# Steps of attention in pairs, a third buffer of probabilities, and a last block in halves

## What is computed

```python
xn = _ln(x, ln1_g, ln1_b)
q, k, v = split(xn @ w_in.T + b_in)              # 16 heads
allowed = (idx % STRIDE == 0)[:, None] | (idx[:, None] == idx[None, :])   # STRIDE = 8
attn = softmax(where(allowed, q @ k.T / sqrt(16), -inf))
x1 = x + (attn @ v) @ w_out.T + b_out
block = x1 + gelu(_ln(x1, ln2_g, ln2_b) @ w1.T + b1) @ w2.T + b2
```

## Time and profile before

| | |
|---|---|
| time, median of 3 runs | 1542.11 us (1539.95 to 1959.27) |
| the profiled execution | 1542.38 us, span 1540.6 us, mean granted clock 0.979 |
| TensorE busy | 1438.3 us, 93% |
| VectorE, ScalarE, GpSimd busy | 835.1, 724.8, 654.2 us |
| attention 0 to 3 | 185.2 to 342.6, 523.3 to 708.1, 885.5 to 1070.3, 1247.2 to 1402.6 us |
| tail | 1402.6 to 1540.6 us |

### The profile page before, as it was taken

One profiled execution on the slowest core, in us unless ns is written; L12 is line 12 of the kernel. 1 busy time (PEld: TensorE's weight loads), 2 busy tenths in 40 slices (PEclk: granted clock), 3 DMA queues, 4 the chain that ended last, 5 costly groups with the idle time before them and its releaser, 6 DMA issues.

```text
span 1540.6 us, 26428 instructions
## 1 busy us (share of the span) xinstructions
PE 1438.3 (93%) x10166; PEld 1077.8 (70%) x10166; DVE 835.1 (54%) x1786; ACT 724.8 (47%) x1071; POOL 654.2 (42%) x536
## 2 busy tenths in 40 slices
PE   4799899999989999999999999999999999999886
PEld 3587655568878765668888866557887865557776
DVE  6655566635745465545646555653664647652331
ACT  3244455553434555554444455454344455554432
POOL 1464411237754422244864431324775422134545
PEclk9899999999999999999999999999999999999999
DMA  7565123205561131212672213220566122300100
GB/s 186 159 197 133 35 47 71 54 16 168 188 161 56 36 75 31 67 43 69 196 205 61 76 24 74 51 52 21 185 191 148 42 55 59 58 24 29 55 1 28
DMA packets 102974, 132.08 MB, mean 86 GB/s; under 512 B 18889, under 2 KB 79249, under 8 KB 99729
## 3 DMA queue, kind: packets, MB, share of 16 engines
q1 hardware_dynamic: 102848, 130.39, 31.3%
HBM read 68.87 MB, written 61.36 MB: 85 GB/s over the span
## 4 chain that ended last, share of the span: by engine, by line
PE 75%; DVE 9%; POOL 5%; SPq 3%; issue 2%; ACT 2%; DMA 2%; POOLq 0%; DVEq 0%; ACTq 0%
PE ps L1370 18%; PE ps L1372 15%; PE ps L1371 15%; PE ps L1546 8%; PE ps L1535 6%; PE ps L1520 5%; DVE mx L1283 2%; PE ps L1591 2%; PE ps L1610 2%; PE ps L1582 2%; POOL rows L922 2%; SPq L747 1%; PE ps L1552 1%; DVE stats L1165 1%; DMA k_d<-kst 1%
## 5 line engine op out<-in xcount | busy, mean ns | idle before, releaser
L1283 DVE TENSOR_REDUCE mx<-ps 128x2 f32<-128x1024 f32 x256 | 313.1, 1223 | 266.6 <-PE ps L1520 252.1
L1033 ACT ACTIVATE prob<-ps 128x1024 f32<-128x1024 f32 x256 | 261.8, 1023 | 155.7 <-PE ps L1535 155.3
L931 POOL TENSOR_TENSOR hid1l<-gel,hid1h 128x512 fp32r<-128x512 f32 x85 | 110.9, 1305 | 233.6 <-ACT hid1h L1075 233.6
L931 POOL TENSOR_TENSOR hid0l<-gel,hid0h 128x512 fp32r<-128x512 f32 x86 | 112.5, 1308 | 226.0 <-ACT hid0h L1075 226.0
L931 POOL TENSOR_TENSOR hid2l<-gel,hid2h 128x512 fp32r<-128x512 f32 x85 | 111.0, 1306 | 223.1 <-ACT hid2h L1075 223.1
L1067 ACT ACTIVATE gel<-ps,cols 128x512 f32<-128x512 f32 x128 | 88.2, 689 | 198.8 <-PE ps L1372 190.3
L1546 PE MATMUL ps<-prob,vals 128*32 128x256 f32 x2048 | 166.3, 397 | 0.0
L1069 ACT ACTIVATE gel<-ps 128x512 f32<-128x512 f32 x128 | 76.5, 597 | 179.7 <-PE ps L1610 179.7
L1535 PE MATMUL ps<-qslot,kslot 50*128 50x256 f32 x1024 | 131.2, 335 | 6.7 <-ACT prob L1033 6.4
L1535 PEld LDWEIGHTS ps<-qslot,kslot 50*128 50x128 f32 x1024 | 77.9, 188 | 73.0 <-issue 47.8
L1520 PE MATMUL ps<-kslot,qslot 48*128 48x512 f32 x512 | 109.7, 424 | 9.0 <-DVE mx L1283 5.9
(11 more groups left out here) (230 smaller groups left out, 3966.7 us busy)
## 6 DMA issues: line engine op xcount, KB each, us to landing
k_d<-kst SPq DMA_DIRECT2D x192, 128.0 KB
kslot<-k_d SPq DMA_DIRECT2D x64, 384.0 KB
xin<-in_L_attn_x SPq DMA_DIRECT2D x32, 256.0 KB, 4.1
x1in<-x_d SPq DMA_DIRECT2D x16, 512.0 KB, 6.8
rows<-xs_d SPq DMA_DIRECT2D x16, 512.0 KB, 5.6
out<-rows SPq DMA_DIRECT2D x16, 512.0 KB, 3.5
y_d<-rows SPq DMA_DIRECT2D x15, 512.0 KB, 3.1
rows<-y_d SPq DMA_DIRECT2D x15, 512.0 KB, 4.3
```

The lines of the kernel that those rows point to most:

```text
L931: nc.gpsimd.tensor_tensor(hid[i % RING][1][:], gel[i % 2][:], hid[i % RING][0][:], ALU.subtract).then_inc(lo_done, 1)
L1033: nc.scalar.activation(prob[(n - 1) % 2][:].rearrange("p e i q -> p (e i q)"), ps[:, 0:2, :].rearrange("p a n -> p (a n)"), ACT.Exp).then_ ...
L1283: nc.vector.tensor_reduce(best[:, :, j % NQ], ps[:, MX:MX + 2, :], AX.X, ALU.max).then_inc(maxr_done, 1)
```

## The change

- Attention: sc and mx of a step stay together, but the weighted sums of two steps stand as one group ahead of the odd step's scores: sc(s), mx(s), at(s-2), at(s-1), sc(s+1), mx(s+1). Both steps of a pair are released together, then three parts of items follow (two where there are two blocks). A third `prob` buffer lies on the two x1 output buffers `x1o`; ACT and GpSimd get waits for that. `ot` is asked for at the second key step everywhere.
- Tail: for batch 3, `opj` writes x1 of tile column 0 straight into `x1in`; only the other half is loaded, and early. `l2a`, `l2b` and the turns move into items 4 to 7 of the first block.
- The last block: sum, statistics, power, normalization (now on VectorE) and store go in halves (`fa`, `fb`).

```diff
-            if p and kk == (1 if len(blocks) == 2 else 3):
+            if p and kk == 1:
...
         def step(s):
+            if s % 2:
+                weighted(s - 3)
+                weighted(s - 2)
             scores(s)
             maxima(s)
-            weighted(s - 1)
             turns(s)
             moves(s)
...
-            while s < STEPS_B and s * 4 * n <= (quarter + ahead) * STEPS_B:
+            while s < STEPS_B and (s - s % 2) * 4 * n // STEPS_B <= quarter + ahead:
...
+        weighted(STEPS_B - 2)
         weighted(STEPS_B - 1)
...
-        items(first, {0: chain[0], 1: chain[1], 2: chain[2], 3: chain[3], 4: [("l2l", middle)], 5: [("ld", middle)], 7: [("l2a", middle)]}, first - 1)
-        put(("l2b", middle))
-        put(("tn", middle, 0))
-        put(("tn", middle, 1))
+        items(first, {0: [("l2l", middle)] + chain[0], 1: chain[1], 2: chain[2], 3: chain[3], 4: [("l2a", middle)],
+                      5: [("ld", middle), ("l2b", middle)], 6: [("tn", middle, 0)], 7: [("tn", middle, 1)]}, first - 1)
...
-        drain()
-        put(("la", last))
-        put(("lb", last))
-        put(("st", last))
+        while pending:
+            i = pending.pop(0)
+            put(("dn", i, 0))
+            put(("dn", i, 1))
+        for h in range(2):
+            put(("fa", h))
+        for h in range(2):
+            put(("fb", h))
...
-        prob = [place(f"prob{i}", [P, 2, 2, QW], F32, m0 + 4096 * i)[0] for i in range(2)]
+        prob = [place(f"prob{i}", [P, 2, 2, QW], F32, at)[0] for i, at in enumerate((m0, m0 + 4096, r1 + 8192))]
...
+                    if n == 0 and bb == LAST:
+                        sp.dma_start(tiles_of(x1in[:])[:, :, 1, :], x1_d[bb, :, :, 1, :]).then_inc(x1ld, 16)
...
+                    if b and PLACE[c] < 2:
+                        pool.wait_ge(av_done, N("at", b - 1, PAIRS - 1, KK - 1))
...
+                    elif a[1:] == (0, 2):
+                        for c in (CHUNKS[-3], CHUNKS[-1]):
+                            k, v = X1_STORE[(b, c)]
+                            act.wait_ge(x1st[k], v)
                     else:
-                        act.wait_ge(av_done, n - 2)
+                        act.wait_ge(av_done, n - 3)
...
+                elif what == "fa":
+                    h = a[0]
+                    pool.wait_ge(fvare_done, h + 1)
+                    nc.gpsimd.tensor_tensor(arstd[:, h, :], avare[:, h, :], mhalf[:, 0:AT], ALU.pow).then_inc(frstd_done, 1)
...
+                    x1 = tiles_of(x1in[:])[:, :, 0, :] if b == LAST else x1g[:]
+                    nc.vector.tensor_tensor(x1, x1g[:], ps[:, BANK[(what, *a)], :].rearrange("p (t d) -> p t d", t=NQ), ALU.add
...
+                elif what == "fa":
+                    h = a[0]
+                    k = len(BLOCKS) - 1
+                    y = rows[ROW_OF[k]][:, 2 * h:2 * h + 2, :]
+                    dve.wait_ge(half_done if h == 0 else down_done, FT * (k + 1))
+                    nc.vector.tensor_tensor(flat(y), flat(y), ps[:, DOWN + h, :], ALU.add).then_inc(fsum_done, 1)
...
+                elif what == "fb":
+                    h = a[0]
+                    y = rows[ROW_OF[len(BLOCKS) - 1]]
+                    dve.wait_ge(frstd_done, h + 1)
+                    for t in range(AT):
+                        at = AT * h + t
+                        nc.vector.tensor_scalar(y[:, at, :], y[:, at, :], amv[:, h, t, 0:1], arstd[:, h, t:t + 1],
+                                                ALU.subtract, ALU.mult).then_inc(fnorm_done, 1)
```

More of the change, by code:

```diff
@@ L21 @@
 KT = D // P
+LAST = B - 1
 FT = F // P
@@ L806, in step @@
                     _, bb, n = BLOCKS[a[0]]
-                    if n == 0:
+                    if n == 0 and bb < LAST:
                         sp.wait_ge(x1gst, 16 * N("stg", bb))
@@ L819, in step @@
                         sp.wait_ge(av_done, N("at", last, PAIRS - 1, KK - 1))
-                    sp.dma_start(tiles_of(x1in[:]), x1_d[bb, :, :, 2 * n:2 * n + 2, :]).then_inc(x1ld, 16)
+                    if n == 0 and bb == LAST:
+                        sp.dma_start(tiles_of(x1in[:])[:, :, 1, :], x1_d[bb, :, :, 1, :]).then_inc(x1ld, 16)
+                    else:
+                        sp.dma_start(tiles_of(x1in[:]), x1_d[bb, :, :, 2 * n:2 * n + 2, :]).then_inc(x1ld, 16)
                 elif what == "ld":
@@ L837, in step @@
                     sp.dma_start(tiles_of(rows[k][:]), src[bb, :, :, 2 * n:2 * n + 2, :]).then_inc(rld[k], 16)
+                elif what == "fb":
+                    h = a[0]
+                    _, bb, n = BLOCKS[-1]
+                    sp.wait_ge(fnorm_done, AT * (h + 1))
+                    sp.dma_start(o_v[bb, :, h, 2 * n:2 * n + 2, :], rows[ROW_OF[len(BLOCKS) - 1]][:, 2 * h:2 * h + 2, :]).then_inc(fst, 16)
                 elif what == "st":
@@ L1329, in step @@
                     dve.wait_ge(xgc_done, N("ldg", b))
-                    nc.vector.tensor_tensor(flat(x1g[:]), flat(x1g[:]), ps[:, BANK[(what, *a)], :], ALU.add).then_inc(x1g_done, 1)
+                    x1 = tiles_of(x1in[:])[:, :, 0, :] if b == LAST else x1g[:]
+                    nc.vector.tensor_tensor(x1, x1g[:], ps[:, BANK[(what, *a)], :].rearrange("p (t d) -> p t d", t=NQ), ALU.add
+                                            ).then_inc(x1g_done, 1)
                 elif what == "l2a":
                     dve.wait_ge(x1ld, 16 * N("l2l", *a))
+                    if PHASE[a[0]][0] == "tail":
+                        dve.wait_ge(x1g_done, N("opj", LAST))
                     ln_a(LN[("l2a", *a)], x1in)
                 elif what == "l2b":
+                    if PHASE[a[0]][0] == "tail":
+                        dve.wait_ge(xsg_done, N("opj", LAST))
                     ln_b(LN[("l2a", *a)], x1in)
@@ L1359, in step @@
                     pick(*a)
+                elif what == "fa":
[3 more added lines that the diff above has]
+                    dve.wait_ge(half_done if h == 0 else down_done, FT * (k + 1))
+                    if h == 0:
+                        dve.wait_ge(xw_done, N("xw", k))
+                    nc.vector.tensor_tensor(flat(y), flat(y), ps[:, DOWN + h, :], ALU.add).then_inc(fsum_done, 1)
+                    dve.wait_ge(fsum_done, h + 1)
+                    for t in range(AT):
+                        nc.vector.bn_stats(astats[:, h, t, :], y[:, t, :]).then_inc(fstat_done, 1)
+                    dve.wait_ge(fstat_done, AT * (h + 1))
+                    for t in range(AT):
+                        nc.vector.bn_aggr(amv[:, h, t, :], astats[:, h, t, :]).then_inc(faggr_done, 1)
+                    dve.wait_ge(faggr_done, AT * (h + 1))
+                    nc.vector.tensor_scalar(avare[:, h, :], amv[:, h, :, 1], EPS, None, ALU.add).then_inc(fvare_done, 1)
+                elif what == "fb":
+                    h = a[0]
+                    y = rows[ROW_OF[len(BLOCKS) - 1]]
+                    dve.wait_ge(frstd_done, h + 1)
+                    for t in range(AT):
+                        at = AT * h + t
+                        nc.vector.tensor_scalar(y[:, at, :], y[:, at, :], amv[:, h, t, 0:1], arstd[:, h, t:t + 1],
+                                                ALU.subtract, ALU.mult).then_inc(fnorm_done, 1)
             for s in STEPS:
```

14 lines of the change are left out of this document (9 added, 5 removed).

## The result

The changed kernel takes 1561 us in the median (1556.6 to 1570.7) beside 1541 for the kernel before: a ratio of 1.0139, 95% interval 1.0113 to 1.0165. The change is some 20 us slower, and 1567 with a range of 1540 to 1592 had been forecast. The profiled execution has a span of 1562.3 us, 21.7 more than before.

The account below looks back on a forecast made before the run. TensorE's own order was taken to set the end in attention. Terms -9 +12.6 +20 +4 +4 -3 -4 = +24.6 us, added to the span of 1540.6 and 1.8 around it, gave 1567 us; range 1540 to 1592.

Parts of the forecast that it names:

- Grouping: Attention: two steps in one group save 0.04 to 0.05 us a pair with maxima; -9 us over all pairs.
- The end of the pair: Attention: items start 2.60 us after a pair's first scores, 0.43 + 0.11 behind the second maxima.
- the second sum: Attention: one weighted sum behind another costs about 0.24 us instead of 0.57.
- rival 1: Attention: grouping pays in full, 0.40 us a pair, 51 us; with the tail, 1484 us; chance 0.05.
- mt without its cover: Attention 0 and 3: turns of negated maxima directly follow turns of blocks and wait longer, 6.3 us a stage, +12.6.
- Bursts: Attention: VectorE's other work falls between pairs and delays reductions, so maxima wait; +20 us, bounds 0 and 40.
- First exponentials: Attention 1 and 2: nothing lies between first and second scores, which wait 1.9 us more each; +4 us.
- Clock: Attention 1 and 2: half clock behind the first exponential's bare wait, 0 to 3.4 us each; +4 us together.
- rival 3: Attention: waits grow into each other or the clock falls there too; above 1590 us; chance 0.10.
- Tail and last block: After attention: x1 skips the trip through memory, -3 us; last block's work in halves, -4 us.
- Third buffer: Attention: second exponential needn't wait for weighted sums, a wait that isn't there now; worth nothing by itself.
- Rival 2: Attention: VectorE's late work is absorbed and the clock holds; +0.6 us, 1543 us; chance 0.25.

Follow-up runs that it names:

- b_pairs: The kernel before with only the edits of attention (steps in pairs, third buffer), its tail as before: 1566.8 us, ratio 1.0171.
- a_tail: The changed kernel with all of attention undone, keeping only the new tail and last block: 1533.3 us, ratio 0.995.
- g_half_after: The changed kernel with exponential and maxima reduction over half of the columns each (doesn't compute the layer): 1512.9 us, ratio 0.9821.
- k_first_apart: The changed kernel with mt ahead of an item's third-part products, and the first two steps of attention 1 and 2 apart: 1526.3 us, ratio 0.9912.
- i_best: The kernel before's attention order with the new tail, mt ahead of third-part products, x1's statistics and turns one item earlier: 1513.7 us, ratio 0.982.
- c_buffer: The kernel before with only the third buffer of probabilities, its index and waits: 1539.3 us, ratio 0.9983.

## Why the prediction was right

**The account.** Forecast: attention +31.6, tail -3, last block -4, in all +24.6. Measured alone: attention +27 (`b_pairs`), tail with last block -6.5 (`a_tail`), and +20 together. The direction and the reason held; three terms inside attention were off, and that the sum came so near is in part luck, since their errors cancel.

**Grouping, -9 forecast, about -19.5 by the rows** (it was not measured alone). The distances were right: scores follow scores after 1.62 to 1.68 us in the pairs, maxima follow maxima after 1.71. The reason for the second was right too; for the first it was only half right, since TensorE's own work is as long (`g_half_after`). The end of the pair was mis-sized. I added 0.11 for late weights to a distance of 0.43 that already had it; and 1.23 from one step's scores to the item was right. The pair takes 2.48 and not 2.60, so 0.16 is saved and not 0.045: 96 x 0.16 = 15.4, and about 4.2 for the pairs without maxima as forecast. The other mistake, 0.24 instead of 0.43 for the second sum, put the end of the sums at 1.47, where it is 1.66. By luck it did not enter the sum: 1.66 lies only 0.04 behind the exponential's 1.62, and the second maxima wait for the reduction until 2.05 in any case. It made rival 1 too good: of its 0.40 a pair, at most 0.18 + 0.14 was ever there.

**mt without its cover, +12.6 forecast, +12.7 measured** (8.8 to 21.5 by line). Behind the turns of a block it waits 1.4 us each time, four times in attention 3, as the waits above show and as predicted.

**Bursts, +20 forecast, +13.1 measured** (5.9 to 19.0; the stage of the earlier trace rows 4.7 instead of 2.4, that of the earlier trace rows 5.0 instead of 0.5). I had 7 a stage. Fewer bursts come late than I placed, and one came later than forecast: where the negated maxima, the sum and the statistics of a block fall into one window, I had 1.3 and it is 2.63. Timelines of attention 1, VectorE and then TensorE:

```profile
608.19 1.09 DVE L1327 CAST negs<-negm 128x4 fp32r<-128x4 f32 x1
...
609.39 1.28 DVE L1389 TENSOR_TENSOR rows<-rows,ps 128x512 f32<-128x512 f32 x2
610.71 1.41 DVE L1196 BATCH_NORM_STATS2 stats<-rows 128x6 f32<-128x256 f32 x4
...
612.64 1.22 DVE L1314 TENSOR_REDUCE mx<-ps 128x2 f32<-128x1024 f32 x1
...
613.92 0.50 PE L1581 MATMUL ps<-kslot,qslot 48*128 48x512 f32 x2 [2.63 <-DVE mx L1314]
```

The reduction before this burst ended at 607.94, the next began at 612.64: 4.7 us of other work in a window of about 2. Of that, 0.9 is a cost that I had not seen at all. The cast of 4 columns takes 1.09 here and 0.17 in the kernel before, and it is no single case. VectorE's groups by line, the kernel before and then the one after:

```profile
L1296 DVE CAST negs<-negm 128x4 fp32r<-128x4 f32 x32 | 5.5, 171 | 1.1
L1327 DVE CAST negs<-negm 128x4 fp32r<-128x4 f32 x32 | 15.4, 482 | 1.1
```

In pairs 12 of the 32 casts are stretched, each beside an operation of GpSimd, and none was before: 9.9 us more on VectorE, in just the windows where it comes late. How much of the 13.1 this is was not tried by itself.

**First exponentials, +4 forecast, +3.6 measured**: 2.6 us each, where it was 0.78. `k_first_apart` gave about 5 for covering them again, so this term may have some clock in it too.

**Clock, +4 forecast, up to +19 measured** (28 against 9, by the windows). This is the largest error. I had it fall only behind the first exponential of attention 1 and 2, by analogy to the earlier trace rows, and held a fall inside attention for the business of rival 3. It falls also behind the longest waits for maxima and behind some shorter waits that follow each other closely. The granted clocks of all executions put the bound for the whole kernel lower, at about 12 us (0.9705 in the median after, 0.978 in the runs of the kernel before beside `a_tail`). The error and that of the grouping, one +15 and the other -10, and the bursts, -7, nearly cancel: 13.1 + 12.7 + 3.6 + 19 - 19.5 = 29, with the clock at its upper bound, and the windows show 26.3.

**Tail and last block, -7 forecast, -6.5 measured.** The sum was right; of its two terms, -4 for the last block came out as -5, and -3 for x1 is not in the waits: TensorE waits 4.7 and 0.7 us there instead of 3.8 and 1.4. POOL and VectorE of the kernel after, then TensorE:

```profile
1447.57 4.85 POOL L945 TENSOR_SCALAR rows<-rows,mv,rstd 128x256 f32<-128x256 f32 x4
1452.39 1.03 POOL L939 TENSOR_TENSOR rstd<-vare,mhalf 128x4 f32<-128x4 f32 x1
1453.53 3.50 DVE L1217 TENSOR_SCALAR x1in<-x1in,mv,rstd 128x256 f32<-128x256 f32 x4 [10.46 <-POOL rstd L939]
...
1457.17 1.08 PE L1643 MATMUL ps<-ident,x1in 128*128 128x128 f32 x4 [4.70 <-DVE x1in L1217]
```

The power does stand behind GpSimd's rows, as forecast. Power and normalization take 4.6 us and not the 3 allowed, so TensorE waits 4.70: the load of x1 was taken off the path, and its place was taken by GpSimd's queue. `i_best` undoes that step, and the wait is gone. What makes up the rest of `a_tail`'s 6.5 is not shown; its tail has a granted clock of 0.96, where before had 0.92. The end came out 1 us better than forecast, 5.0 from first sum to end (8.0 instead of 13.0). The first half's sum starts at 1554.22, the second half's power at 1558.12, and what is left behind it are two normalizations of 0.74 together and the store.

**Third buffer, 0 forecast, 0 measured** (`c_buffer`).

**The rivals.** Rival 1 fails on its own sign: no second scores started under 1.62 us after the first. Rival 2 fails since the waits for maxima rose to about 5 a stage. Rival 3's price was not reached, although its reason, the clock inside attention, was the right one.

## What to carry to other kernels

Before two steps are put together, write down for each buffer with one copy when it comes free within the pair: the gain ends there, whatever the shapes cost. Put TensorE's own time in the group beside it, from a row of the grouped shape: here it was as long as the exponential's. Then look for every other operation whose wait the separate step covered; here one small turn of 128 by 8 that lost its cover cost more, with the clock behind it, than the grouping saved, and three lines that moved it gave 30 us back. Look also at which operations of two engines the new order makes run at the same time. A wait is to be priced together with the waits near it, because of what the clock may do next.

## What the runs showed of the hardware

- A second group of weighted sums behind a first costs 0.43 us to the next shape, and a single one 0.57: sixteen products on 32 columns have more of their time in themselves than I gave them, and a change of shape less.
- Products that had to wait for their bank reach the next shape after 0.43 us instead of 0.32: the second maxima of a pair in the kernel after and in `g_half_after`.
- TensorE's granted clock fell to 0.50 for 3 to 10 us behind single waits of 2.6 us, and twice behind waits of 1.1 and 1.4 us that lay 2 us apart. Both also occurred without a fall, the second kind twice in the same trace.
- Operations of VectorE can stretch beside GpSimd's: four normalizations of 256 columns took 1.38 us in the kernel before, with GpSimd idle, and 3.50 in the kernel after, where GpSimd works meanwhile; the cast of 4 columns took 0.17 or up to 1.10. In the kernel after, none of the 56 such normalizations of x1 and none of the 18 casts that met no operation of GpSimd took longer than 0.42 and 0.17. Not every one that met it was slower, and no run took GpSimd's work away.
